# Moving the first turn of an attention pipeline into the last steps of a scan, and splitting its last feed forward by sequence

## The reference

```python
xn = _layernorm(x)
# branch s: xz = xn @ W_in; depthwise convolutions of both halves with silu; x_dbl = xs @ W_xdbl
def step(h, inp):                      # selective scan, 16 states for each of 128 channels
    d_t, u_t, B_t, C_t = inp
    h = exp(d_t[..., None] * A) * h + (d_t * u_t)[..., None] * B_t[:, None, :]
    return h, einsum('bdn,bn->bd', h, C_t)
# y = scan + u * D ; s = concat(y, z) @ W_out + b_out
# branch g, for each of DEPTH = 6 layers (16 heads of 64 channels, window 32):
x = attn_layer(shift_tokens(x), ...) + x     # q, k normalised, rotated, local softmax, @ Wo
x = ffn_layer(shift_tokens(x), ...) + x      # layernorm, W1, a * gelu(gate), W2
# shift_tokens: channels 64..127 come from the token before, in each sequence
out = x_in + s * silu(g)
```

## Time and profile before

| | |
|---|---|
| median of 3 runs | 3661.58 us (3657.19 to 3663.26) |
| profiled execution | 3656.87 us, its span 3655.1 us |
| first stage | about 0 to 309 us |
| first turn | 309.9 to 364.2 us |
| the 48 items | to about 3626 us |
| after the last output projection | 3625.9 to 3655.1 us |
| busy over the span | PE 93%, DVE 88%, ACT 82%, POOL 79% |

### The profile page before, as it was taken

How to read it: one execution, slowest core, us unless ns; L and a number is a source line. 1 busy time by engine, 2 the same in 40 slices (tenths; PEclk the granted TensorE clock), 3 DMA queues, 4 the chain that set the end, 5 groups by cost and what they waited for, 6 DMA issues and landing times.

```text
span 3655.1 us, 95521 instructions
## 1 busy us (share of the span) xinstructions
PE 3410.4 (93%) x30848; PEld 2173.2 (59%) x30848; DVE 3201.7 (88%) x11632; ACT 3009.3 (82%) x8806; POOL 2875.0 (79%) x2385
## 2 busy tenths in 40 slices
PE   7886899999999999999999999999999999999997
PEld 3443566666666666666666666666666666666664
DVE  7995998888898898898888898988988988988985
ACT  6552888888888888888888888888888888888886
POOL 6885887788787788787788787788787788887883
PEclk9997999999999999999999999999999999999999
DMA  5442332233332233332333332333322332322322
GB/s 168 133 134 86 109 108 97 104 119 104 108 110 97 103 117 107 110 106 97 106 116 104 114 107 97 104 118 104 112 104 97 106 118 102 117 102 99 107 100 88
DMA packets 261725, 396.41 MB, mean 108 GB/s; under 512 B 45550, under 2 KB 86572, under 8 KB 261228
## 3 DMA queue, kind: packets, MB, share of 16 engines
q1 hardware_dynamic: 261228, 390.30, 31.3%
HBM read 157.91 MB, written 6.03 MB: 45 GB/s over the span
## 4 chain that ended last, share of the span: by engine, by line
PE 51%; DVE 23%; POOL 9%; issue 9%; ACT 6%; DMA 2%; SPq 1%; DVEq 0%; POOLq 0%; ACTq 0%
PE bank L793 9%; DVE ab L1410 7%; PE bank L782 6%; PE bank L754 5%; PE bank L327 5%; PE bank L329 5%; PE bank L328 5%; DVE sm L1455 4%; PE bank L736 4%; PE bank L821 4%; PE bank L763 3%; DVE wide L1343 3%; POOL rot L1202 3%; POOL pr L1194 3%; PE bank L764 2%
## 5 line engine op out<-in xcount | busy, mean ns | idle before, releaser
L1044 ACT ACTIVATE pr<-sm,nb,rq 128x128 f32<-128x128 f32 (+1 forms) x3072 | 1517.3, 501 | 11.8 <-DVE nb L1461 11.5
L1194 POOL TENSOR_TENSOR pr<-pr,rden 128x640 f32<-128x640 f32 x768 | 963.7, 1255 | 495.2 <-DVE rden L1435 493.4
L1410 DVE TENSOR_TENSOR ab<-bank,ltab 128x512 f32<-128x512 f32 x1536 | 984.6, 683 | 106.7 <-PE bank L329 83.6
L1202 POOL TENSOR_TENSOR rot<-ab,swp 128x512 f32<-128x512 f32 x768 | 984.8, 1282 | 102.4 <-DMA swp<-ab 101.9
L1455 DVE CUSTOM_DVE_ANT_0 sm<-bank,mask 128x128 f32<-128x128 f32 (+1 forms) x3072 | 841.3, 331 | 37.6 <-PE bank L754 36.8
L1044 ACT ACTIVATION_READ_ACCUMULATOR pr<-sm,nb,rq 128x1 f32 x3072 | 596.9, 194 | 0.0
L754 PEld LDWEIGHTS bank<-rot 64*64 64x64 f32 x12288 | 287.7, 132 | 431.9 <-issue 337.5
L1442 DVE COPY pt<-bank 128x512 f32<-128x512 f32 x768 | 531.5, 692 | 10.3
L1208 POOL TENSOR_TENSOR rot<-rot,rkb 128x512 f32<-128x512 f32 x384 | 490.8, 1284 | 51.4 <-DMA rkb<-k_scratch 51.0
L1032 ACT ACTIVATE sq<-bank 128x512 f32<-128x512 f32 x768 | 452.2, 589 | 72.9 <-DVE ab L1410 66.2
L782 PE MATMUL bank<-pt,vtok 128*64 128x160 f32 (+1 forms) x6144 | 461.2, 292 | 27.1 <-ACT vtok L1058 27.1
(11 more groups left out here) (181 smaller groups left out, 6152.1 us busy)
## 6 DMA issues: line engine op xcount, KB each, us to landing
swp<-ab SPq DMA_DIRECT2D x1536, 128.0 KB, 2.0
rkb<-k_scratch SPq DMA_DIRECT2D x768, 128.0 KB, 2.9
rot<-c_scratch SPq DMA_DIRECT2D x64, 256.0 KB, 3.3
sq<-c_scratch SPq DMA_DIRECT2D x64, 256.0 KB, 3.2
xs<-xT SPq DMA_DIRECT2D x95, 128.0 KB, 2.3
xs<-xT SPq DMA_DIRECT2D x95, 127.5 KB, 2.4
raw<-Wqkv SPq DMA_DIRECT2D x48, 128.0 KB, 2.5
wo<-Wo SPq DMA_DIRECT2D x6, 512.0 KB, 4.8
```

The costliest lines, as they stand in the source:

```text
L1044: ins = act.activation(pr[:, s % 4, i, t, 0:P + WINDOW * t], sm[:, s % 2, i, cs], ACT.Exp, bias=nb[:, s, t, i:i + 1], scale=head_scale(rq, ...
L1194: ins = pool.tensor_tensor(pr[:, e % 4, :, :, :], pr[:, e % 4, :, :, :], rden[:, e, :, :].rearrange("p t i -> p i t").unsqueeze(3) .to_bro ...
L1202: pool.tensor_tensor(rot[:, PAIRS * (j % 2) + j // 2, :], ab[:, j % 2, 0, :], swp[:, j % 2, :], ALU.add).then_inc(qk_rot, 1)
L1410: ins = dve.tensor_tensor(seqs(ab[:, j % 2, i, :]), seqs(use_bank("qk", j)[:, :]), ltab[:, 2 * (j % 2) + i:2 * (j % 2) + i + 1, :] .to_bro ...
```

## The change

**State stage.** Chunk 5 of the weights is split at step 22 of the scan (ACT and POOL), chunk 7 is loaded at step 26. The matrices that spread B, which lay in the second half of the v weights, now lie in the second buffers of `xh` and `xl`, and W_out lies in `pt`. The shifted copy and the split of group 0 are made during the last group by SP, ACT and POOL; the six DVE instructions for it and two bank memsets are gone.

**First turn.** The end of the state layer is sent within the first turn: pairs 6 and 7 at step 1, `state_out` at step 3, `skip` at step 2, its copy on ACT at step 4, its store at step 6, the splits of chunks 6 and 7 at steps 3 and 6. PE waits for m_scan before block 0. The blocks rotate over banks 4, 5 and 0, and products and swaps have four slots (`wide` and `gg` lend two each). The second turn waits for m_sout (PE) and m_sdma (ACT).

**The end.** In "drain" silu of groups 0 to 3 is at step 1, of 4 to 6 at step 3, the seven multiplications at step 4. Two transposed groups stand before the last output projection, two between centring and variance, three behind the variance, on five banks. The last residual, centring, norm, down projection, silu, multiplication, transposition and store go by sequence (256 columns). The token shift is made by two matmuls with half of the centring matrix each (`ltab`), not by DMA; DVE does what POOL did in the norm.

```diff
-EARLY_AT = {10: 2, 12: 3, 14: 4, 17: 5, 19: 6}
+TAIL = {"pairs": 1, "out": 3, "skip": 2, "out_sb": 4, "store": 6, "split": (3, 6)}
+EARLY_AT = {10: 2, 12: 3, 14: 4, 17: 5, 19: 6, 26: 7}
-EARLY = 5
+EARLY = 6
+SPLIT_AT_STEP = {1: 0, 3: 1, 5: 2, 7: 3, 9: 4, 22: 5}
-BACK = {"load": 10, "silu": 5, "mul": 8, "transpose": 9, "add": 9, "store": 12}
+BACK = {"load": 10, "silu": {1: (0, 4), 3: (4, 7)}, "mul": 4, "halves": 3, "before": 2, "between": 4, "add": (8, 10, 11), "store": 12}
+BACK_BANKS = (0, 1, 2, 3, 5)
+LAST_BANKS = {"cen": (7, 4), "var": (6, 7), "dn": (4, 7), "out": (2, 3)}
...
+        def qk_bank(j, lead):
+            return bank[(4, 5, 0)[j % 3]] if lead else use_bank("qk", j)
+        def ab_of(j, i, lead):
+            k = j % 4 if lead else j % 2
+            return ab[:, k, i, :] if k < 2 else wide[:, 2 * (k - 2) + i, :]
+        def swp_of(j, lead):
+            k = j % 4 if lead else j % 2
+            return swp[:, k, :] if k < 2 else gg[:, k - 2, :]
...
             state_groups(pe, group)
-            for k in (6, 7):
-                add_pair(k, GROUPS - 1)
-            state_out(GROUPS - 1, 1, False)
-
-            pe.wait_ge(m_sout, GROUPS)
+            pe.wait_ge(m_scan, D_STATE * GROUPS)
...
+            def last_centre(x):
+                pe.wait_ge(cen_halves, 1)
+                for b in range(GB):
+                    c0 = x * GT + b * SEQ
+                    pe.wait_ge(at_add, ITEMS + b + CREDIT)
+                    pe.matmul(last_bank("cen", b)[:, one_seq(b)], ltab[:, 0, 0:P], xT[:, c0:c0 + SEQ], start=True, stop=True,
...
+                    pe.matmul(last_bank("cen", b)[:, b * SEQ + 1:b * SEQ + SEQ], ltab[:, 1, 0:P], xT[:, c0:c0 + SEQ - 1],
...
                 for s in range(16):
+                    if first and s == TAIL["pairs"]:
+                        for k in (6, 7):
+                            add_pair(k, GROUPS - 1)
+                    if first and s == TAIL["out"]:
+                        state_out(GROUPS - 1, 1, False)
...
+                    if kind == "drain" and s == AT["wo"] + NWO - 1:
+                        for g in range(BACK["before"]):
+                            turn_back(g)
                     if AT["wo"] <= s < AT["wo"] + NWO and prev is not None:
                         project_out(s - AT["wo"], prev)
...
+                    lead = n16 + 16 * q == CREDIT
+                    if lead and j >= 4:
+                        dve.wait_ge(qk_rot, n16 + j - 3)
+                    elif not lead:
                         dve.wait_ge(qk_rot, n16 + (16 * q + j - 1))
```

More of the change, by code:

```diff
@@ L469, in turn @@
                 prev2, prev, cur, nxt = o
+                first = nxt is not None and cur is None
                 nk, n2, n8, n16 = n.z[64], n.n[2], n.n[8], n.n[16]
@@ L522, in turn @@
                         shift_next(gs[2])
-                    if s == AT["shift"] and prev is not None:
+                    if s == AT["shift"] and prev is not None and kind != "drain":
                         shift(prev)
@@ L837, in bank_work @@
                             q_norms(i, q, bk)
+                        elif what == "cen" and kind == "drain":
+                            last_centre(gs[1])
+                            for g in range(BACK["before"], BACK["between"]):
+                                turn_back(g)
                         elif what == "cen":
                             centre(q, bk)
+                        elif what == "var" and kind == "drain":
+                            last_variance()
+                            for g in range(BACK["between"], GROUPS - 1):
+                                turn_back(g)
                         elif what == "var":
                             variance(q, bk)
+                        elif what == "g" and i == 0 and kind == "drain":
+                            last_up(bk)
                         elif what in ("g", "a"):
@@ L1091, in turn @@
                     split_high(nl, 6)
+                if prev is None and cur is not None:
+                    act.wait_ge(m_sdma, 16 * GROUPS)
                 for s in range(16):
+                    if first and s == TAIL["out_sb"]:
+                        state_out(GROUPS - 1)
+                    if first and s in TAIL["split"]:
+                        split_high(0, EARLY + TAIL["split"].index(s))
                     if s % 2 == 0 and s < 6 and prev is not None:
@@ L1233, in turn @@
                 for s in range(16):
+                    if first and s in TAIL["split"]:
+                        split_low(0, EARLY + TAIL["split"].index(s))
                     if s < 2 and prev is not None:
@@ L1487, in turn @@
                         products(15, cur)
[L1488 removed]
+                    if s == AT["residual"] and kind == "drain":
+                        last_residual(gs[1])
+                    if s == AT["residual"] and prev is not None and kind != "drain":
                         residual(prev)
@@ L1505, in turn @@
                     for role, _ in due("residual2", s):
-                        if group_of(role, o) is not None:
+                        if group_of(role, o) is not None and kind != "end":
                             residual2(group_of(role, o))
```

281 lines of the change are left out of this document (200 added, 81 removed).

## The result

The changed kernel takes 3623.32 us (median of 4 runs, 3620.12 to 3623.68), the kernel before 3659.39 (4 runs, 3657.11 to 3663.26): a ratio of 0.9898, 95% interval 0.9884 to 0.9913. The prediction was 3624. The profiled execution of the change is one of 3623.43 us with a span of 3621.6, 33.5 less than the span before. One execution of a later kernel, the one with the new end alone, took 9684 us, far from its other nine, and is left out of the comparison.

What follows compares the result with a forecast made beforehand. At the seam rings of waits bound, at the end one chain over all engines. 0 - 29.5 + 0.5 - 7.1 + 0.2 - 1.5 = -37.4 us gives 3619.5 profiled, 4.7 more for the median: 3624 us, range 3613 to 3636.

Steps and rivals of the forecast that it cites:

- State stage: Term for the splits added in the state stage: 0 us, bounds 0 and one whole split, 1.3 us.
- block 0 before 302 us: Sign at the start of the first turn: block 0 projected before 302 us.
- Seam: Last scan to second turn: first scores 30.2 us earlier, next turn's products about 0.7 later; -29.5 us, bounds -36 and -22.
- the walk: First-turn blocks followed queue by queue (DVE, SP, POOL): product 12 ends at 327.5 us, first scores start at 334.0.
- 1.3 to 1.6 us a block: Sign in the first turn: products at this pace from 312 us on.
- The rival on PE's clock: PE's clock stays at half in the first turn, PE needing 28.5 us from block 3: +7, so 3631; chance 0.13.
- Above 0.9 from 300 to 334: Sign in the first turn: PE's granted clock above 0.9 from 300 to 334 us.
- The rival on SP: SP's queue of 43 DMAs bounds the first turn, adding 5 to 8 us: 3630; chance 0.12.
- without a gap between 320 and 334: Sign in the first turn: SP without a gap between 320 and 334 us.
- The middle: First scores to last output projection: same 3259.7 us as before, within 2; wrong if longer by more than 3.
- Slower by a kept phase: Later turns keep the second turn's changed phase; some 47 take 1 us longer each: 3671 us; chance 0.03.
- The end: After last head outputs: transposes +0.5, residual to up projection -7.1, first `gated` +0.2, down projection onward -1.5 us.

Runs made afterwards that it cites:

- the end alone: The kernel before with only the new end, its seam and first turn unchanged: median 3651.6 us, ratio 0.9976 to the kernel before.
- swaps on two queues: Changed kernel, with ACT instead of SP issuing the second DMA of each first-turn swap: median 3621.2 us, ratio 0.9897 to the kernel before.
- PE busy before scores: Changed kernel plus 14 unread passes on PE ahead of the second turn's first scores: median 3622.7 us, ratio 0.9900 to the kernel before.
- splits later: Changed kernel with the splits of the last two chunks at steps 8 and 12, not 3 and 6: 3622.2 us, ratio 0.9898 to the kernel before.
- PE busy at the sums: Changed kernel plus 6 unread PE passes ahead of the first turn's second sums of squares: 3618.9 us, ratio 0.9890 to the kernel before.
- the old banks: Changed kernel with the first turn's banks of the kernel before instead of three in turn: 3629.9 us, ratio 0.9915 to the kernel before.

## Why the prediction was right, and where it was not

- **The sum.** -37.4 us predicted; the medians differ by 36.1, the two spans by 33.5. The 2.6 between the two would fit the heaps of the last scan, as the profiled execution of before is in the early one and that of the change in the late one; in which the other executions were is not known. That 3623.3 met 3624 so closely is in part luck: the profiled execution was to come to 3619.5 and took 3623.43, and the 4.7 us from there to the median, which three runs of before had suggested, made up for it.
- **State stage, 0 with bounds 0 and 1.3.** Measured +2.04, outside; but the same shift stands in a kernel that has none of this stage's edits, so nothing speaks against the term of 0. Its bounds were of the wrong kind: they should have held what one trace differs from the next in this stretch. The sign "block 0 before 302 us" was missed by it, at 302.77.
- **Seam, -29.5.** First scores -29.4 where -30.2 was written; the prediction's "0.7 us later" of the next turn became 2.2 by the third turn's eighth step (-27.2). Inside the walk errors cancel. The pair was to end 3.9 us behind the end of the last scan and ended 1.4 later, since PE had stood 3.3 us for the scan and worked at half clock (0.74 in 304 to 310); `state_out` took 1.3 in line instead of 3.6, at full clock; the stretch from product 3 to 12 took 0.9 more, where the half clock at step 8 alone cost 1.3; and from product 12 to the first scores it was 7.8 instead of 6.5, as swap 12 left SP 1.7 us behind its product and landed after 0.55 us of idle POOL. The sign "1.3 to 1.6 us a block" was missed: 15.9 us for nine blocks are 1.77, and the walk's own 15.0 are 1.67.
- **The rival on PE's clock** (chance 0.13, +7 us) happened in small: the clock was half for some 3 us (0.50 in 321 to 324), not for 13 blocks, at a price of 1.3 us. "Above 0.9 from 300 to 334" was wrong. So was "never stands longer than about 2 us": PE stood 3.27 for the scan and 4.50 ahead of the first scores. The rival's 28.5 us come out with 1.3 us a block, passes back to back at half clock, and not with the 1.7 that it names.
- **The rival on SP** (0.12, 3630) cost 1.1 us. SP had no gap from 325.0 to 335.9, but stood from 323.0 to 325.0, so that the sign "without a gap between 320 and 334" was missed; its queue decided rotations 10 and 12.
- **The middle, within 2 of 3259.7.** Measured 3263.1, which by the prediction's own sign, 3 us, was to mean that it is wrong. Of the 3.4 more, 2.2 fell ahead of the third turn's eighth step: 0.7 in the second turn, and 1.5 where PE's sums at the turn's end ran at half clock behind a wait of 1.76 us. In the kernel before, the same wait left the clock full. The change, then before:

```profile
399.74 1.94 PE L826 MATMUL bank<-sq,headsum 128*32 128x512 f32 x8
```

```profile
426.18 1.06 PE L736 MATMUL bank<-sq,headsum 128*32 128x512 f32 x8
```

  These 2.2 are the loss of the seam from 29.4 to 27.2, and stand in no kernel with the old first turn: the end alone takes 87.8 us to that step from its first scores, before 88.0, the change 90.2. Behind that step the end alone took longer than the change with the code of before (3174.2, 3170.9, before 3169.8), so the other 1.2 are within what traces differ by, and a threshold of 3 us was below that.
- **Slower by a kept phase** (0.03): no turn is longer for it. From the third turn's eighth step on all fourteen kernels take 3169.3 to 3174.4, whatever their first turn.
- **The end.** Residual to up projection: -7.1 predicted, -7.5 measured. From the up projection to the end of the span (the terms of -1.5 and +0.2 together): -1.3 and -1.9, since the last store is shorter by 0.4 and not by 0.1. The transposes ahead of the output projection: +0.5 and +0.1, just below its bound of 0.2: PE stood there 0.70 for ACT's copy anyway, and 8 transposes at full clock took no more than 0.93.

## What to carry to other kernels

Where no engine is full, count the rings: way round divided by depth for each, and undo one at a time, as both can matter though only one seems to bind. Look at the granted clock behind the waits of PE: a wait can be paid twice when products behind it are on the path, as one of 2.05 us was here; work that nobody reads, put into the wait, was a cheap test and a cheap cure (1.3 us). And before a shift of 2 us in an untouched stretch is explained, look at the same stretch in a kernel whose code there is the same.

## What the runs showed of the hardware

- The granted clock behind a wait of PE: half behind 2.05 to 2.11 us (changed kernel, swaps on two queues, PE busy before scores), full behind 1.64 us (splits later) and behind 0.66 (PE busy at the sums); behind 1.76 us once full and once half; and with the old banks full behind 2.08 us and half behind 1.29. The wait just before does not settle the clock by its length.
- One and the same operation of 4 elements a lane on DVE took 0.36 us (before) or 1.20 (change): in both it ended with the operation that POOL was in.
- In 14 traces, one for each kernel, the last scan starts at 299.2 to 299.6 or at 301.0 to 301.8, with nothing in between; both the old state stage and the new one occur at both places.
- 16 DMAs issued by ACT behind its squares instead of by SP cost the first turn nothing that shows: the first scores came at 34.2 us instead of 35.3.
